# The third tile of a mixture-of-experts gather, transposed with fewer rows and columns

## The reference

```python
logits = xt @ gate_w                       # 1024 x 8
top_p, top_i = lax.top_k(softmax(logits), 2)
for k in range(2):                         # cap = 160 tokens an expert and k
    buf = ...at[e, pos_c].set(xt * keep)   # tokens gathered by expert
    h = gelu(einsum('ecd,edf->ecf', buf, w1) + b1)      # 256 -> 1024
    y = einsum('ecf,efd->ecd', h, w2) + b2              # 1024 -> 256
    y = y + gelu(buf @ wd) @ wu                         # rank 32
    out = out + tok * keep * w
out = out + 0.2 * shared(xt)               # a ninth expert that sees all tokens
```

## Time and profile before

| | |
|---|---|
| median of 3 runs | 180.77 us (180.49 to 181.28) |
| profiled execution: span, first to last instruction | 179.5 us |
| around the span (median less span) | 1.27 us |
| instructions | 4056 |
| PE busy | 174.6 us (97%) |
| PEld (weight loads) busy | 170.0 us |
| DVE, ACT, POOL busy | 148.4, 145.8, 97.4 us |

### The profile page before, as it was taken

The page is one execution under the profiler, slowest core; times in us unless marked ns, Lnnn a source line. Parts: engine busy times, 40 slices in busy tenths (PEclk is TensorE's granted clock), DMA queues, the critical chain, the costliest instruction groups (busy, mean ns, idle before and its releaser), DMA issues.

```text
span 179.5 us, 4056 instructions
## 1 busy us (share of the span) xinstructions
PE 174.6 (97%) x1410; PEld 170.0 (95%) x1410; DVE 148.4 (83%) x332; ACT 145.8 (81%) x323; POOL 97.4 (54%) x110
## 2 busy tenths in 40 slices
PE   5999999999999999999999999999999999999994
PEld 6987789999989999999999999999999999999993
DVE  5678999999876779979789699798899889889822
ACT  3379799706779898997899799899899899898930
POOL 5802368210647662087977858958946455164700
PEclk9999999999999999999999999999999999999999
DMA  4594001669828492696878758579597868776242
GB/s 134 151 346 142 0 2 50 201 194 328 268 52 302 112 316 70 227 252 95 279 237 122 285 171 158 188 257 188 137 318 164 231 222 148 248 218 92 31 71 84
DMA packets 25885, 31.84 MB, mean 177 GB/s; under 512 B 4572, under 2 KB 22392, under 8 KB 25864
## 3 DMA queue, kind: packets, MB, share of 16 engines
q1 hardware_dynamic: 21720, 26.22, 45.5%
q0 software_dynamic: 3904, 5.25, 16.9%
q10 hardware_dynamic: 240, 0.10, 0.2%
HBM read 26.31 MB, written 5.24 MB: 176 GB/s over the span
## 4 chain that ended last, share of the span: by engine, by line
PE 88%; DVE 6%; ACT 3%; issue 1%; another core or an unknown queue 1%; POOL 0%; DVEq 0%; POOLq 0%; ACTq 0%
PE y_ps L1038 13%; PE y_ps L1040 13%; PE y_ps L1039 13%; PE hid_ps L1038 8%; PE hid_ps L1040 8%; PE hid_ps L1039 8%; PE turn_ps L1038 4%; PE turn_ps L1040 4%; PE turn_ps L1039 4%; PE y_ps L1046 2%; DVE w_l L703 2%; PE turn_ps L1207 2%; ACT gelu_f L627 1%; ACT hid_h L628 1%; PE hid_ps L1066 1%; PE turn_ps L1066 1%
## 5 line engine op out<-in xcount | busy, mean ns | idle before, releaser
L733 DVE TENSOR_TENSOR hid_l<-gelu_f,hid_h 128x320 fp32r<-128x320 f32 (+2 forms) x88 | 42.8, 501 | 13.8 <-ACT hid_h L628 13.4
L477 POOL DMA_INDIRECT out_rows<-y_row,slot_tok x23 | 38.2, 1662 | 26.8 <-DVE y_row L929 11.9
L463 POOL DMA_INDIRECT slot_in<-slot_rows,slot_src x23 | 33.0, 1435 | 18.5 <-DVE slot_src L889 8.2
L1038 PE MATMUL y_ps<-w_h,hid_h 128*128 128x256 f32 x128 | 36.4, 284 | 0.3 <-DVE hid_l L733 0.3
L1039 PE MATMUL y_ps<-w_l,hid_h 128*128 128x256 f32 x128 | 36.2, 283 | 0.0
L1040 PE MATMUL y_ps<-w_h,hid_l 128*128 128x256 f32 x128 | 36.2, 283 | 0.0
L1038 PE MATMUL hid_ps<-xs_h,w_h 128*128 128x256 f32 (+2 forms) x96 | 27.9, 291 | 0.0
L627 ACT ACTIVATE gelu_f<-hid_ps,bias_s 128x320 f32<-128x320 f32 x48 | 26.1, 543 | 1.9 <-PE hid_ps L1040 1.3
L1039 PE MATMUL hid_ps<-xs_l,w_h 128*128 128x256 f32 (+2 forms) x96 | 27.5, 287 | 0.0
L1040 PE MATMUL hid_ps<-xs_h,w_l 128*128 128x256 f32 (+2 forms) x96 | 27.5, 287 | 0.0
L710 DVE TENSOR_TENSOR w_l<-w_raw,w_h 128x512 fp32r<-128x512 f32 x40 | 26.6, 701 | 0.0
(11 more groups left out here) (239 smaller groups left out, 446.2 us busy)
## 6 DMA issues: line engine op xcount, KB each, us to landing
w_raw<-in_L_ffn_w SPq DMA_DIRECT2D x16, 1024.0 KB
w_raw<-in_L_ffn_sw SPq DMA_DIRECT2D x3, 1024.0 KB
x_in<-in_x SPq DMA_DIRECT2D x2, 512.0 KB, 3.7
w_raw<-in_L_ffn_sw SPq DMA_DIRECT2D x2, 512.0 KB, 7.1
slot_rows<-token_row SPq DMA_DIRECT2D x2, 512.0 KB, 4.1
wu_raw<-in_L_ffn_wu SPq DMA_DIRECT2D x24, 32.0 KB
out_rows<-base SPq DMA_DIRECT2D x1, 512.0 KB
slot_in<-slot_rows,slot_src POOLq DMA_INDIRECT x23
```

Source lines behind the costliest of these rows:

```text
L463: pool.indirect_dma_start(out=slot_in[par][0:n, s, :], out_offset=None, in_=x_rows, in_offset=bass.IndirectOffsetOnAxis(ap=slot_src[0:n, e ...
L477: pool.indirect_dma_start(out=out, out_offset=bass.IndirectOffsetOnAxis(ap=slot_tok[0:n, e, s:s + 1].bitcast(U32), axis=0), in_=y_row[0:n, ...
L733: dve.tensor_tensor(hid_l[:, j - 1, 0:n], gelu_f[:, j % 3, 0:n], hid_h[:, j - 1, 0:n].bitcast(F32), ALU.subtract).then_inc(hid_split, 1)
L1038: pe.matmul(out_ap, l_h, r_h, start=start, stop=False)
```

## The change

`turn_slots` is given the number of columns that the expert's matmuls will use, in place of the number of tiles. The number of transposes stays. The third one of each half now takes only as many rows of `slot_in` as are left, n = size - 256, and the unit matrix is cut to n x n, so that it writes n columns. With the rows that were never gathered no longer read, the two memsets are taken out, and the waits on `consts` go from 12 to 10.

```diff
-            for i in range(2):
-                pool.memset(slot_in[i][:, ST - 1, :], 0.0).then_inc(consts, 1)
...
-                pool.wait_ge(consts, 12)
+                pool.wait_ge(consts, 10)
...
-            def turn_slots(e, par, tiles):
+            def turn_slots(e, par, size):
...
-                    for s in range(tiles):
-                        ins = pe.transpose(turn_ps[k][:, s * P:(s + 1) * P], slot_in[par][:, s, k * P:(k + 1) * P],
-                                           ident[:, :])
+                    for s in range((size + P - 1) // P):
+                        n = min(P, size - s * P)
+                        ins = pe.transpose(turn_ps[k][:, s * P:s * P + n], slot_in[par][0:n, s, k * P:(k + 1) * P],
+                                           ident[0:n, 0:n])
...
-                    shared_out(h, 1, lambda: turn_slots(0, 0, ST))
+                    shared_out(h, 1, lambda: turn_slots(0, 0, SLOTS))
...
-                        turn_slots(e + 1, other, (sizes[e + 1] + P - 1) // P)
+                        turn_slots(e + 1, other, sizes[e + 1])
```

More of the change, by code:

```diff
@@ L787, in choose @@
                 if k == 0:
-                    dve.wait_ge(consts, 12)
+                    dve.wait_ge(consts, 10)
                 else:
@@ L1193, in rows_out @@
                     ins.then_inc(y_made, 1 + (TILES[e] - len(tiles) if s == tiles[0] else 0))
-            def turn_slots(e, par, tiles):
+            def turn_slots(e, par, size):
                 pe.wait_ge(slots_in[par], 16 * sum(TILES[par:e + 1:2]))
                 if e == 0:
-                    pe.wait_ge(consts, 12)
+                    pe.wait_ge(consts, 10)
                     pe.wait_ge(slots_sided, 1)
```

## The result

The changed kernel takes 183.44 us (median of 16 runs) against 180.93 for the kernel before beside it; the ratio is 1.0118 with a 95% interval of 1.0087 to 1.0149, that is 1.6 to 2.7 us slower. A second comparison of the same two gave 1.0124 (1.0066 to 1.0182). The forecast was 1.7 us slower. Apart from three long ones, the times of either kernel lie in two groups with nothing between them, and by the lower group alone the medians are 182.65 us (8 of 16 runs) and 180.83 (12 of 16), 1.8 us apart.

A forecast was written before the change was run, and what follows sets the result against it. PE was taken to bound the kernel: 0.3 us for expert 0 plus 1.38 for experts 1 to 3, memsets nothing, made 1.7 us on 180.77, so 182.5 us. The range was 181.1 to 183.3.

The forecast's parts named there:

- PE bounds the run: From first expert's start to last quarter's end, PE queue time moves the end one for one; PE busy 97%.
- 0.45 us for 16 rows, 0.48 for 32, 0.53 for 64: Added PE time per expert's slot turn from its two short third-tile transposes, by their row count.
- The drain at 64 rows: Expert 0's 64-row transposes were assumed to stop the pulled-ahead load like 16 or 32 rows, about 0.09 us both ways.
- Expert 0: 0.3 of its 0.53: Expert 0's turn, in the shared layer's last row: 0.53 us longer, 0.3 reaching the end; bounds 0 and 0.53.
- PE's side: Before expert 0's first hidden tile: PE arrives 0.53 us later, less 0.2 idle time there, leaving 0.3.
- DVE's side: DVE's xs_l for expert 0: last transpose about 0.3 us late, less 0.13 cover, so DVE some 0.2 late.
- The memsets at nothing: Dropping POOL's two zero memsets, 0.55 us at 5.81 to 6.36, was costed at nothing; at most 0.5 us gain.
- One way only: Rival: drain only on leaving the short shape, 0.15 us an expert, about 0.5 us, 181.3; chance 0.10.
- no drain: Rival: load behind a short transpose starts with it; 0.05 us an expert saved, 180.6; chance 0.10.
- 64 rows exempt: Rival: drain for 16 and 32 rows but not 64, expert 0 adds nothing; 1.4 us, 182.2; chance 0.12.
- longer drains: Rival: drains last to the recorded end, 0.12 us more per short tile; 2.6 us in all, 183.4; chance 0.08.
- The sum: Whole kernel: 0.3 for expert 0 plus 1.38 for experts 1 to 3 gives 1.7 us slower, 182.5 us.

The follow-up runs named there:

- the two kernels with an extra transpose later on: Kernel before plus a repeated second-tile transpose in each half for experts 4 to 7: 64 rows, ratio 1.0144; 128 rows, one run, 181.51 us.
- short ones side by side: Changed kernel with the short transposes of both halves put behind the four full ones; ratio to the kernel before 1.0067.
- 72 rows: Change with memsets kept and the third tile of experts 0 to 3 turned with 72 rows and columns; ratio to the kernel before 1.0008.
- 65 rows: Change with memsets kept and the third tile of experts 0 to 3 turned with 65 rows and columns; one run, 181.1 us.
- 65 rows, third tile first: As the 65-row kernel, with the third tile turned first in each half; ratio to the kernel before 0.9995, median 180.75 us against 180.92.
- the two experiments that leave that turn alone: Kernel before with an extra second-tile transpose in each half for experts 4 to 7, of 64 rows (ratio 1.0144) or 128 (181.51 us).
- the kernel with the extra 64-row transposes: Kernel before, with the second tile's first 64 rows turned again in each half for experts 4 to 7; ratio 1.0144.
- the two halves of the change: Kernel before, memsets kept, with short shapes for expert 0 alone (ratio 1.0033) or for experts 1 to 3 alone (ratio 1.0078).

## Why the prediction was right

The stretch with the four turns, from the first transpose for expert 0 to the first for expert 4:

| kernel | stretch, us | above 53.49 |
|---|---|---|
| before, profile (with its lag of DVE) | 53.66 | |
| before, as in the two kernels with an extra transpose later on | 53.49 | |
| changed, both profiles | 55.23, 55.22 | 1.74 |
| short shapes for expert 0 only | 53.84 | 0.35 |
| for experts 1 to 3 only | 54.89 | 1.40 |
| changed, memsets put back (1.3 of it PE's two waits) | 56.60 | 3.11 |
| short ones side by side | 54.22 | 0.73 |
| 72 rows | 53.28 | -0.21 |
| 65 rows, profile with a lag of DVE like that of before | 53.45 | -0.04 |
| 65 rows, third tile first | 53.17 | -0.32 |

- **PE bounds the run.** Right: what the turns of experts 1 to 3 lost (1.40) was all there at expert 4's turn.
- **0.45 us for 16 rows, 0.48 for 32, 0.53 for 64.** Measured 0.45 and 0.45 for experts 2 and 3; 0.53 for expert 0; for expert 1, 1.400 less 0.915 (the two experiments that leave that turn alone) is 0.485. The gap of 0.09 us after the stream, read off the gate's eight transposes, held before all eight short loads of the changed kernel (idle times of 0.17 us), and the load behind a short one came 0.16, 0.17 to 0.18 and 0.20 us after it with 16, 32 and 64 rows.
- **The drain at 64 rows.** No row of before showed it. It is there, and 65 rows have none. The Trainium skill, "TensorEngine Tiling (Array Packing)", section Tiling Modes, states the rule, a drain at each change of mode: the trace agrees, with one gap at each change between 128 rows and 64, 32 or 16, and none between two short transposes side by side. A change among the short ones (64 to 32, say) was not run.
- **Expert 0: 0.3 of its 0.53.** Measured 0.35. PE's side is as argued: 0.53 less an idle time of 0.19. DVE's side was sized too small. The prediction let it be late by 0.2, behind a cover of 0.13 us between ACT's first copy and DVE. That copy took 0.44 us and ended at 54.19, so the cover in that profile was 0.08, and where DVE is not behind there is almost none. In the kernel with the extra 64-row transposes, whose first transpose starts at 52.25, ACT and DVE ran so:

```profile
53.10 0.77 ACT L632 ACTIVATE xs_h<-turn_ps 128x320 fp32r<-128x320 f32 x2 [1.28 <-PE turn_ps L1207]
53.58 0.89 DVE L907 TENSOR_TENSOR xs_l<-turn_ps,xs_h 128x320 fp32r<-128x320 f32 x2 [0.36 <-ACT xs_h L632]
```

DVE's xs_l starts 1.33 us after the first transpose there and 1.66 in the changed kernel (54.03 - 52.37), so it is 0.33 late and not 0.2. The two counts tie, and which of them holds PE the runs don't tell. That the second one was no longer than the first, and so left the sum right, is luck.
- **The memsets at nothing.** Right: POOL's next copy started at the same time, and the two halves of the change, both with memsets, add up to 1.75 against 1.74 without them.
- **The rivals.** "One way only" fell with the gaps before all eight short loads, "no drain" with those and the ratio, "64 rows exempt" with expert 0's turn, and "longer drains" with 0.45.
- **From expert 4 on as before.** Right for the turns. In the first profile of the changed kernel PE stood 0.15 us longer at 160.2, before expert 7's outputs; it did not in the second, so I don't count it as the change's. What it waited for I did not find out.
- **The sum.** Forecast 1.7, the profiles' 1.74, the comparisons' 2.1 and 2.2. The last lie 0.4 to 0.5 higher, and 1.74 is inside their intervals. By the lower groups of the result section the first comparison gives 1.8, and the second, read the same way, 182.45 - 180.81 = 1.6. So the excess comes of a larger part of the changed kernel's runs in the upper group; whether the change does that or chance, so few runs don't tell.

## What to carry to other kernels

Where PE bounds a kernel, look at the row count of every matmul that is to be made smaller. Here shapes of 64, 32 and 16 rows between 128-row neighbours stopped the pulled-ahead weight load on both sides and cost more than the columns they saved: the turns with 65 rows were 0.04 us shorter than before, the turn with 64 rows was 0.53 us longer. If small shapes can't be avoided, put them side by side, so that the change is paid once for the group (0.20 us a turn instead of 0.45). And price such a step from rows of the same trace that have the same neighbours: eight transposes of another tile, a hundred lines away, gave the cost of a turn to within 0.01 us.

## What was unexpected

Part of the spread of the timings, for whichever kernel, seems to arise in the first ten microseconds. Warm-up and condition product in the changed kernel's profile, and in that of the kernel with short shapes for experts 1 to 3:

```profile
7.13 1.28 PE L1054 MATMUL y_ps<-ones 128*128 128x128 bf16 x20
8.25 2.00 PE L1064 MATMUL hid_ps<-cond_diag,x_in 128*128 128x128 f32 x16
```

```profile
7.50 2.34 PE L1056 MATMUL y_ps<-ones 128*128 128x128 bf16 x20
9.64 2.53 PE L1066 MATMUL hid_ps<-cond_diag,x_in 128*128 128x128 f32 x16
```

The same twenty matmuls took (9.64 - 7.50) / 20 = 0.11 us each instead of (8.25 - 7.13) / 20 = 0.06. The first matmul of the shared layer's hidden tiles began at 13.71 instead of 11.79, and expert 0's turn at 54.50 instead of 52.37. The ratio is that of the two levels of TensorE's clock (1.2 and 2.4 GHz), but the granted clock of the stretch from 7 to 12 us reads 1.00 in both, so that it is the clock is not shown. The profile of the kernel with the short ones side by side shows it too (2.34 us, turn at 54.53). These two profiles are of runs in the upper group of their kernel. What decides between the two I did not try; it is about the size of the effect studied here, which is why the readings above rest on stretches of the trace as well as on ratios.
